# A two-layer cross-attention kernel with mixtures of experts: the experts of layer 0 issued in longer pieces

## What is computed

```python
router_weights = softmax(xf @ rw + rb)
topw, topi = top_k(router_weights, 2)
combine = zeros((T, 8)).at[arange(T)[:, None], topi].add(softmax(topw))
h = gelu(einsum('td,edf->etf', xf, w1) + b1[:, None, :], approximate=False)   # 8 experts, 128 -> 512
eo = einsum('etf,efd->etd', h, w2) + b2[:, None, :]                            # 512 -> 128
out = einsum('etd,te->td', eo, combine)
```

## Time and profile before

| | us |
|---|---|
| median of 3 runs | 5684.33 |
| lowest and highest of them | 5668.9, 5712.68 |
| the profiled execution's own time | 5729.6 |
| its span in the profile | 5728.3 |

### The profile page before, as it was taken

How to read it: one execution, slowest core, us unless ns; L and a number is a source line. 1 busy time by engine, 2 the same in 40 slices (tenths; PEclk the granted TensorE clock), 3 DMA queues, 4 the chain that set the end, 5 groups by cost and what they waited for, 6 DMA issues and landing times.

```text
span 5728.3 us, 101447 instructions
## 1 busy us (share of the span) xinstructions
PE 5172.3 (90%) x41312; PEld 2859.7 (50%) x41312; DVE 3500.2 (61%) x6335; ACT 2781.6 (49%) x5505; POOL 640.9 (11%) x660
## 2 busy tenths in 40 slices
PE   5888888888888888888899999999999999999999
PEld 2455445555445554445444455444555445554456
DVE  4665555555555555555556666666666666666664
ACT  1565455554555555555544444444444444444444
POOL 1111111101111101111011110101101011010100
PEclk7799888888888888888889999999999999999999
DMA  2122112221112211112222222222222222222221
GB/s 56 32 47 51 40 37 51 51 46 48 38 40 55 51 43 47 35 46 66 66 60 61 72 75 62 74 64 67 76 63 76 64 71 69 66 79 56 68 52 61
DMA packets 167977, 326.98 MB, mean 57 GB/s; under 512 B 25656, under 2 KB 76624, under 8 KB 167520
## 3 DMA queue, kind: packets, MB, share of 16 engines
q1 hardware_dynamic: 167520, 320.49, 22.6%
HBM read 237.40 MB, written 4.19 MB: 42 GB/s over the span
## 4 chain that ended last, share of the span: by engine, by line
PE 43%; DVE 4%; ACT 1%; POOL 1%; issue 1%; SPq 0%; DMA 0%; DVEq 0%
PE sums L695 8%; PE a L657 8%; PE d L771 5%; PE a L665 5%; PE a L759 5%; PE d L679 3%; DVE d L810 2%; PE d L733 1%; PE d L580 1%; PE a L607 1%; PE d L727 1%; PE d L600 1%; PE a L640 1%; PE d L613 1%; PE d L631 1%
## 5 line engine op out<-in xcount | busy, mean ns | idle before, releaser
L966 ACT ACTIVATE probs_c<-a 128x512 f32<-128x512 f32 (+1 forms) x3584 | 1834.0, 563 | 2329.6 <-PE a L665 2327.2
L803 DVE TENSOR_REDUCE chunk_max<-d 128x2 f32<-128x808 f32 x1024 | 1005.4, 998 | 621.7 <-PE d L679 618.5
L810 DVE CUSTOM_DVE_ANT_0 d<-d,mcross_q 128x808 f32<-128x808 f32 x1024 | 1023.1, 1012 | 506.7 <-PE d L679 504.0
L695 PE MATMUL sums<-probs_c,vc 128*32 128x256 f32 x13312 | 1154.9, 421 | 13.0 <-PEq L1233 12.9
L679 PE MATMUL d<-kc,qc 24*128 24x404 f32 x4096 | 1095.0, 442 | 27.8 <-DVE chunk_max L803 9.3
L665 PE MATMUL a<-qc,kc 25*128 25x256 f32 (+1 forms) x6656 | 948.1, 346 | 177.0 <-ACT probs_c L966 146.1
L665 PEld LDWEIGHTS a<-qc,kc 25*128 25x128 f32 (+1 forms) x6656 | 557.4, 191 | 902.1 <-issue 440.2
L771 PE MATMUL d<-w_back,hidden 128*128 128x128 f32 x4352 | 617.9, 301 | 32.3 <-DVE chunk_max L810 26.7
L771 PEld LDWEIGHTS d<-w_back,hidden 128*128 128x128 f32 x4352 | 570.0, 211 | 94.2 <-DVE chunk_max L810 35.7
L657 PE MATMUL a<-mcross_k,ident_b 128*128 128x512 bf16 (+1 forms) x1792 | 549.1, 378 | 14.8 <-ACT probs_c L966 14.8
L759 PE MATMUL a<-xT_e,w_in 128*128 128x256 f32 x2176 | 534.2, 390 | 19.9 <-ACT hidden L985 19.9
(11 more groups left out here) (157 smaller groups left out, 4635.9 us busy)
## 6 DMA issues: line engine op xcount, KB each, us to landing
w_in<-in_experts SPq DMA_DIRECT2D x272, 256.0 KB, 2.8
w_back<-in_experts SPq DMA_DIRECT2D x272, 256.0 KB, 3.1
kc<-k_hi SPq DMA_DIRECT2D x1024, 50.0 KB
ctxT<-in_ctxT SPq DMA_DIRECT2D x32, 800.5 KB, 5.7
kc<-k_lo SPq DMA_DIRECT2D x512, 50.0 KB
mask_words<-in_mcross SPq DMA_DIRECT2D x32, 800.5 KB
mask_words<-in_mcrossT SPq DMA_DIRECT2D x32, 768.0 KB
out_x<-xe SPq DMA_DIRECT2D x32, 128.0 KB, 1.8
```

What stands on the lines that cost most here:

```text
L695: last = pe.matmul(acc[HP * j:HP * j + HP, :], T["vc"][x.p][0:x.kn, v0:v0 + HP], probs_of(T, x)[0:x.kn, j, half:half + S], start=x.j == 0, ...
L803: done = dve.tensor_reduce(T["chunk_max"][:, x.g % 2, x.i, x.j:x.j + 2, x.c], tile[:].rearrange("p (h n) -> p h n", h=2)[:, :, 0:CHUNK], A ...
L810: done = dve.tensor_tensor_reduce(both, both, mask, 1.0, -3e38, ALU.add, ALU.max, T["chunk_max"][:, x.g % 2, x.i, x.j, x.c:x.c + 1])
L966: act.activation(probs_of(T, x)[0:x.kn, x.j, 0:n], tile[0:x.kn, 0:n], ACT.Exp, scale=SCALE).then_inc(M["a_read"], 1)
```

## The change

In layer 0 the single items of a pair are put into one item. In the first pair it is EF0 EF0 EF1 EF1 ES0; in the others it is EFe EFe ES(e-1) EF(e+1) EF(e+1) ESe; ES7 stays alone at the end. The loads stand inside the items, each still behind the step that frees its slot. No instruction is added or removed. Layer 1 is left as it was.

```diff
         if l == 0:
             for e in range(0, count, 2):
-                out.append(self.hidden(l, p, e) + self.hidden(l, p, e + 1))
+                piece = self.hidden(l, p, e)
+                if e:
+                    piece += self.expert_out(l, p, e - 1)
+                    piece += self.load_expert(l, e + 1, 1)
+                piece += self.hidden(l, p, e + 1)
                 for one in (e, e + 1):
-                    out += self.load_expert(l, one + 2, 0) if one + 2 < count else []
-                for one in (e, e + 1):
-                    out += self.expert_out(l, p, one)
-                    out += self.load_expert(l, one + 2, 1) if one + 2 < count else []
+                    piece += self.load_expert(l, one + 2, 0) if one + 2 < count else []
+                piece += self.expert_out(l, p, e)
+                piece += self.load_expert(l, e + 2, 1) if e + 2 < count else []
+                out.append(piece)
+            out += self.expert_out(l, p, count - 1)
```

## The result

The changed kernel takes 5503.44 us (median of 4 executions, 5489.11 to 5533.73), the kernel before 5682.61 us (4 executions, 5668.9 to 5712.68) in the same job. The ratio is 0.9685, with a 95% interval of 0.9624 to 0.9745: 3.1% faster, where 1.8% was forecast.

A forecast was written before the change was run, and what follows sets the result against it. TensorE's stream bounds the kernel, with waits and time at 1.2 GHz in layer 0. Against the median, (4.2 waits + 2.3 clock) x 16 rounds = 104 us, so 5684 - 104 = 5580 us; range 5480 to 5680.

The forecast's parts named there:

- rival 4: Layer 0 rounds settle like the early one of 163.9 us and lose the waits too: 5500 us; chance 0.1.
- Step 1: TensorE's waits behind and inside the four bursts of a round in layer 0 go: -6.4 us a round.
- Step 2: Beats that lose their ES wait for probabilities again, in layer 0: +2.2 us a round.
- Step 3: Three stretches at 1.2 GHz behind bursts vanish: -3.6 us a round, counted as -2.3 against the median.
- Step 4: Moved ES and loads hold nothing up in layer 0's queues: no cost; a load stall would be 3.1 us.
- Step 5: VectorE gets no MC for 8 us in place of 4 at each burst, but is idle, not late: nothing.
- Rival 1: Waits go, but the low clock stays elsewhere in layer 0's rounds: 67 us gained, 5617 us; chance 0.2.
- Rival 3: Beats without ES between and behind pieces fall to 1.2 GHz: 93 us slower, 5777 us; chance 0.12.

The follow-up runs named there:

- Tanh runs: Tanh in place of Gelu in layer 0, so no table switch: 5465 us in the order of the kernel before, 5489 us in the changed order.
- fair pair: No edit: second profiles of the kernel before (5588.7 us) and the changed kernel (5506.8 us), rounds of both with 27.3 us at 1.2 GHz.
- both ES behind: Against the changed kernel, the four EF stay together and both ES of the same pair follow directly: 5564 us, 5560 us when run again.
- pieces of four: The changed kernel's pieces joined two by two, giving two pieces of four experts a round and half the table switches: 5567 us.

## Why the prediction was right, point by point

The mechanism was right: an ES behind the EF covers the switch back to Exp, and the waits at the bursts went. That the total came out right as well is partly luck. Of the 104 us forecast, 67 were waits and 37 the clock. Of the 107 us measured against all executions, 94 are in a and 10 in the clock: 27 us too little in one term, 27 too much in the other. And the 5503 us itself lies nearer to rival 4's 5500, which had a chance of 0.1, than to 5580.

*Step 1, the waits at the bursts, -6.4 us.* Right but for one. No matmul of L764 waits for a Gelu, and three of four pieces end without a wait over 0.25 us. The second keeps 0.91 us, since the sum left out that a transpose's copy can stand between Gelu and Exp. The Tanh runs show that the switch is the cause: with Tanh in the changed order the wait behind that piece is 0.20 us.

*Step 2, the lost cover, +2.2 us.* Somewhat too much. Waits for probabilities went from 9.5 to 6.3 us a round, not by 5.2: 2.0 us came back, 0.9 of it the wait of the second piece. Steps 1 and 2 together were 4.2 x 16 = 67 us, and against the first profile the page's idle time fell by just that (47 + 20). In the two profiles with equal time at 1.2 GHz all idle time of TensorE fell by 5.3 us a round and by 80 us in all. The 16th round, to which I gave the same gain, had no waits behind its bursts.

A term was missing: the busy time of TensorE, for which I counted no change, fell by 1.5 us a round. Over the kernel that is some 20 us: the busy time of 5021.6 us is 2.3 less than the 5023.9 of the kernel before, with 45 us more at 1.2 GHz, which cost 18. These 20 and the 80 us of idle time are the 100 us by which a differs between these two executions (94 in the mean of all). Part of the 1.5 us can be read from starts. An ES among the beats of the kernel before, and the matmuls behind it:

```profile
887.72 2.05 PE L771 MATMUL d<-w_back,hidden 128*128 128x128 f32 x16
889.70 0.64 PE L695 MATMUL sums<-probs_c,vc 128*32 128x256 f32 x8
```

A piece of the changed kernel at 2.4 GHz:

```profile
1309.34 1.89 PE L764 MATMUL a<-xT_e,w_in 128*128 128x256 f32 x8
1311.07 1.95 PE L776 MATMUL d<-w_back,hidden 128*128 128x128 f32 x16
1312.86 1.89 PE L764 MATMUL a<-xT_e,w_in 128*128 128x256 f32 x8
1314.59 1.95 PE L776 MATMUL d<-w_back,hidden 128*128 128x128 f32 x16
1316.46 0.64 PE L700 MATMUL sums<-probs_c,vc 128*32 128x256 f32 x8
```

From its start to the next start the ES among beats took 1.98 us, those of the piece 1.79 and 1.87; over the eight ES of a round that is an estimate of 1 us. The whole piece is 7.1 us where I had 7.7. I had taken durations and never asked what a neighbour does to them. But this is argued from one piece, and the Tanh pair does not bear it out: there the changed order has a 10 us higher a. The cause of the missing term stays open.

*Step 3, the clock, -2.3 us against the median.* This is the term that was mis-sized. Against all executions it measured 25 us at 1.2 GHz, 10 us of time, 0.6 us a round; against the four of the first job it may have been 83 us, 5.2 us a round, worked back from their times. The place was half right. No low stretch lies directly behind a piece, as I expected, but 6.8 us came ahead of and in the first half of the second piece, and 3.4 at the start of the fourth, where I had counted on gapless matmuls over the whole array. In the fair pair the total stayed at 27.3 us a round. What vanished against the first profile is above all 17 us of self-attention, and they are gone from the second profile of the kernel before too. My price of 0.35 us for each us at 1.2 GHz was not far off (0.41 over 54 executions); the amount was guessed from three rows, in a quantity that swings by 458 us from one execution of the same kernel to the next.

*Step 4, order and queues, nothing.* Right: no L776 row waits for a load or a Gelu, its idle time of 25.8 us is layer 1's. *Step 5:* nearly right: TensorE's idle time ahead of the MC rose only from 26.7 to 34.0 us over the kernel, less than the 0.7 us a round that step 2 allowed for it.

*The rivals.* Rival 1 is what all 54 executions of the kernel before would say of the mechanism: the waits gone, the low clock much as it was (757 and 732 us). Its price of 67 us was too small for the 94 in a. Rival 3, beats without ES at 1.2 GHz, did not happen in this order; but with both ES behind, and with pieces of four, something of its kind did: 175 to 180 us more at 1.2 GHz than in the changed kernel, about 73 us of time. Which feature of an order makes that is **open**. It is not the sum of the waits, as they were fewer there. Rival 4 is what the first job's figure and the profile show, for a reason it had named: rounds like the one of 163.9 us, less the waits (157.0 us measured, where it had 159.7). In the chances, half of rival 1 is 0.10, not 0.12, so the 0.70 for faster should have been 0.68.

## What to carry to other kernels

Where a wait is an engine's switch of function tables, put work of the waiting engine behind the last activation before the switch back, enough for the rest of the activations and the load; a matmul that is ready anyway will do, and a copy that slips between the two functions undoes part of it. When TensorE's clock is not at its full level all the time, take time and clock of many executions of both kernels in the same job, split each into a part at full clock and a part at the low one, and judge an order by the first before believing a ratio. Neither fewer waits nor longer dense pieces alone promise the full clock.

## What the runs showed of the hardware that I had not expected

The same program settles at rounds of 174.1 us, or mostly at 163.8 us with some of 160.5 between, with 56, 27 or 20 us of each at 1.2 GHz; in the settled rounds the low stretches stand at the same places each time. The same self-attention instructions, with waits of 0.6 to 0.8 us ahead of them, took 17 us at 0.50 in one profile of the kernel before and 11 us at 1.00 in the other. In the changed kernel the eight issues over the whole array at the start of the second piece ran at 1.2 GHz, without a gap: 3.78 us, where they take 1.89 at 2.4 GHz. 18 us of added TensorE work made the median of the kernel before 17 us longer, with rounds that mostly alternate between 162.9 and 168.2 us.
